# Twelve identity matmuls ahead of the first tile, contiguous first loads on two DMA queues, and the products with ahi first in every tile

## The chip, the cores and the metric

The kernel runs on one core of one Trainium2 chip. The metric is the device time of one execution in microseconds (us), as the median of several executions. Three executions of the kernel before took 613.04, 613.05 and 613.65 us. All durations below come from one profiled execution, which took 613.1 us. Its trace spans 611.3 us, so 1.8 us lie outside the span.

## The reference, cut to what matters

A graph layer with two branches and a residual, then a second graph layer. `adj` is a full 4096x4096 float32 matrix, and the features are 4096x128.

```
# layer 0, for (x, W1, b1) and for (x2, W2, b2)
ax = adj @ x;  h = ax + (1 + eps) * ax
for i in range(3): h = relu(h @ W[i].T + b[i])
x = layernorm(x + concat(h1, h2) @ Wm.T + bm)
# layer 1
A = adj + eye;  d = rsqrt(sum(A, axis=1))
x = layernorm(x + (d[:, None] * A * d[None, :] @ x) @ W.T + b)
```

So `adj` is multiplied once with x and x2 (256 columns) and once with the normalised x (128 columns).

## The kernel before

**Three products for one.** Every float32 operand is split in a rounded part and a rest. ScalarE (ACT) copies a tile `raw` (128x1024) to `ahi` in the rounded format fp32r (L489), VectorE (DVE) subtracts to get `alo` (L636). TensorE (PE) then adds up x_hi·ahi, x_hi·alo and x_lo·ahi (L344) in PSUM, 512 columns at a time. In layer 0 a tile is 2 branches x 3 products x 2 halves = 12 matmuls, in layer 1 it is 6.

**Order of the work.** The output columns are cut in four quarters of 1024. For each quarter, 32 tiles of `adj` (n = 0 to 31) are added up. Layer 0 runs quarters 0 to 3, then layer 1 runs quarters 0 to 3. The small dense layers of a quarter (L362, L373), the residual, the statistics and the norm are placed at fixed tiles of the next quarter. DVE also adds up row sums in layer 0 (L644, L647, L651).

**Rings.** `ahi` and `alo` have four places (SPLIT = 4): ACT may round tile n when PE has finished tile n - 4 (`block_used`). SyncE (SP) issues the loads of `adj`, two tiles in one DMA, when DVE has used the old ones.

**Waits of PE.** Before a tile PE waits for both `hi_ready` and `lo_ready`:

```
if not first:
    wait(pe, hi_ready, at)
    wait(pe, lo_ready, at)
...
w, a = ((whi, hi), (whi, lo), (wlo, hi))[k]
```

Middle tiles go through the branches b, then k = 0, 1, 2, then the halves c. Tiles 0 and 31 finish one PSUM bank after the other.

**The start.** SP issues x piece 0 (the first two blocks of x and of x2, 256 KB, L259), then the two halves of tile 0 of `adj` (256 KB each, L266), tile 1 (512 KB, L267), x piece 1, and so on. Pieces of x go through ACT (L464) and DVE (L622) and must be split before tiles 0, 2, 4, 8, 16 and 24; DVE splits piece 3 behind its work for tile 7. In tile 0 PE waits for `alo` of each half (L630). GpSimd (POOL) builds an identity (L899, L901), which layer 1 adds to `adj` (L791).

Of the kernel before, what the change touches and what calls it, by code (L numbers as in the profile page):

```python
# [27 lines left out]
P = 128  # L28
N = 4096
QUARTERS = 4  # L30
QW = N // QUARTERS
# [30 lines left out]
PE_MERGE = (10, 7)  # L62
PE_PROJECT = 1


# [25 lines left out]
X_PIECE_AT = {KB * q + k: i for i, (q, k, _) in enumerate(X_PIECES)}  # L91

X_AFTER = {1: 1, 3: 2, 7: 3, 12: 4, 20: 5}


def build(nc, a_t, x12, params, out):
    with ExitStack() as ctx:
# [103 lines left out]
        const_step = sem("const_step")  # L201
        const_ready = sem("const_ready")
        gain_ready = sem("gain_ready")
        whi_ready = sem("whi_ready")
        wlo_ready = sem("wlo_ready")

        as_f32 = lambda ap: ap.bitcast(F32)

        def wait(eng, s, value):
# [41 lines left out]
        def _(sp):  # L251
            def load_x(i):
                q, k0, k1 = X_PIECES[i]
                if q == 2:
                    sp.wait_ge(x_split, 2 * 3)
                if q == 3:
                    sp.wait_ge(x_split, 2 * 4)
                place = 2 * (q % 2)
                sp.dma_start(xn[:, place:place + 2, k0 * P:k1 * P],  # L259
                             x12[q][:, :, k0 * P:k1 * P]).then_inc(x_in[i], 16)  # L260


            load_x(0)
            for c in range(CH):
                cols = slice(c * CW, (c + 1) * CW)
                sp.dma_start(raw[:, 0, 0, cols], a_t[0][:, 0, cols]).then_inc(half_in[c], 16)  # L266
            sp.dma_start(raw[:, 0, 1], a_t[0][:, 1]).then_inc(raw_in[0], 16)  # L267
# [52 lines left out]
        def _(pe):  # L320
            def products(q, layer, n, stationary, first_wait):

                at = q * JB + (layer * QUARTERS * JB + n + 1)
                banks = [(b, c) for b in range(len(stationary)) for c in range(CH)]
                hi = [ahi[:, n % SPLIT, c * CW:(c + 1) * CW] for c in range(CH)]
                lo = [alo[:, n % SPLIT, c * CW:(c + 1) * CW] for c in range(CH)]
                first = isinstance(at, int) and at == 1
                if not first:
                    wait(pe, hi_ready, at)
                    wait(pe, lo_ready, at)  # L330
                if n in (0, JB - 1):

                    order = [(b, c, k) for b, c in banks for k in range(3)]
                else:
                    order = [(b, c, k) for b in range(len(stationary)) for k in range(3) for c in range(CH)]
                for b, c, k in order:
                    whi, wlo = stationary[b]
                    w, a = ((whi, hi), (whi, lo), (wlo, hi))[k]
                    bank = b * CH + c
                    if n == 0 and k == 0:  # L340
                        first_wait(bank)
                        if first and b == 0:
                            pe.wait_ge(lo_half if c == 0 else lo_ready, 1)
                    mm = pe.matmul(ps[bank][:, :], block_of(w, n), a[c],  # L344
                                   start=(n == 0 and k == 0), stop=(n == JB - 1 and k == 2))
                    if n == JB - 1 and k == 2 and (b, c) != banks[-1]:
                        mm.then_inc(ay_done if layer else ax_done, 1)
                mm.then_inc(block_used, 1)
# [40 lines left out]
            def layer0_quarter(q, before):  # L389
                def empty(bank):  # L390
                    if before is not None:
                        wait(pe, h_ready, before * (4 * M) + (bank + 1))
                for n in range(JB):
                    if before is None and n in X_PIECE_AT:
                        pe.wait_ge(x_split, 2 * (X_PIECE_AT[n] + 1))
# [14 lines left out]
            def last_products(q):  # L410

                for c in range(CH):
                    for n in range(JB - SPLIT, JB):
                        if c == 0:
                            pe.wait_ge(hi_ready, (QUARTERS + q) * JB + n + 1)
                            pe.wait_ge(lo_ready, (QUARTERS + q) * JB + n + 1)
# [10 lines left out]
            def layer1_quarter(q, before):  # L427
# [31 lines left out]
        def _(act):  # L459
            def round_x(i):  # L460
                q, k0, k1 = X_PIECES[i]
                act.wait_ge(x_in[i], 16)
                for b in range(2):
                    act.activation(x_hi_parts[b][:, q, k0 * P:k1 * P], xn[:, 2 * (q % 2) + b, k0 * P:k1 * P],  # L464
                                   ACT.Copy).then_inc(x_hi, 1)

            def round_a(q, layer, n):

                p = n // 2
                if layer == 0:  # L470
                    start = isinstance(q, int) and q == 0 and p < RAW
                    if start and n == 0:
                        for c in range(CH):
                            act.wait_ge(half_in[c], 16)
                            act.activation(ahi[:, 0, c * CW:(c + 1) * CW], raw[:, 0, 0, c * CW:(c + 1) * CW],
                                           ACT.Copy).then_inc((hi_half, hi_ready)[c], 1)
                        return
                    if start and n % 2 == 0:
# [112 lines left out]

            round_x(0)
            layer0_quarter(0, None)
# [23 lines left out]
        def _(dve):  # L617
            def split_x(i):
                q, k0, k1 = X_PIECES[i]
                for b in range(2):  # L620
                    dve.wait_ge(x_hi, 2 * i + b + 1)
# [228 lines left out]

            split_x(0)
            layer0_quarter(0, None)
# [34 lines left out]
        def _(pool):  # L887
# [5 lines left out]
            def norm_power(done, r=slice(0, KB)):  # L893
# [65 lines left out]
```

## Time and profile before

| what | value |
|---|---|
| median of 3 executions | 613.05 us (613.04 to 613.65) |
| profiled execution, its span | 613.1 us, 611.3 us |
| PE busy | 590.3 us, 97% of the span |
| DVE busy | 545.6 us, 89% |
| ACT busy | 368.2 us, 60% |
| DMA read from HBM | 139.14 MB |
| chain that ended last | PE 85%, DVE 10%, ACT 2%, issue 2%, DMA 1% |

Engines run side by side, so busy times don't add up. A matmul's busy time includes its passage through the array, and successive ones overlap: the distance from start to start is what a matmul costs. The chain goes back from the last instruction, each time to what released it.

### The profile page before, as it was taken

The numbers are of one execution on the slowest core, as the hardware profiler recorded it, in microseconds if no ns is written. First come the engines' busy times: TensorE is split into PE (matmuls) and PEld (weight loads), VectorE is DVE, ScalarE is ACT, GpSimd is POOL, SyncE is SP. The second block draws the span as 40 slices with busy tenths as digits, with TensorE's granted clock in tenths as the row PEclk, the third lists the DMA queues.
The fourth block names the chain that finished last, engine by engine and source line by source line (L and its number), as shares of the span: only waits on it lengthen the run. The fifth ranks groups of instructions, "written<-read, shape, count | busy, mean of one in ns | idle before, by whom it ended". The sixth has DMA issues, their size and how long they took to land.

```text
span 611.3 us, 7947 instructions
## 1 busy us (share of the span) xinstructions
PE 590.3 (97%) x2636; PEld 478.9 (78%) x2636; DVE 545.6 (89%) x696; ACT 368.2 (60%) x443; POOL 28.1 (5%) x30
## 2 busy tenths in 40 slices
PE   4999999999999999999999999999989999999994
PEld 3888888888888888888888888858668778778873
DVE  5999989998987997998899999876898998998994
ACT  5555337752545773453675254685767797797781
POOL 1000000001100000200000110001100100000011
PEclk9999999999999999999999999999999999999998
DMA  8967555334555433455533576583978999999800
GB/s 292 414 234 281 205 203 206 138 138 138 207 206 183 161 137 137 169 191 191 204 137 137 206 275 248 172 335 139 339 283 346 342 399 363 349 380 371 333 34 36
DMA packets 21289, 141.55 MB, mean 232 GB/s; under 512 B 2320, under 2 KB 2832, under 8 KB 5008
## 3 DMA queue, kind: packets, MB, share of 16 engines
q1 hardware_dynamic: 20544, 139.15, 61.1%
q10 hardware_dynamic: 720, 2.10, 0.9%
q8 instruction: 13, 0.21, 0.1%
q14 instruction: 12, 0.10, 0.0%
HBM read 139.14 MB, written 2.10 MB: 231 GB/s over the span
## 4 chain that ended last, share of the span: by engine, by line
PE 85%; DVE 10%; ACT 2%; issue 2%; DMA 1%; POOL 1%; POOLq 0%; SPq 0%; DVEq 0%; ACTq 0%
PE ps L344 75%; DVE alo L636 7%; PE pd L362 6%; PE pd L373 2%; PE pd L405 1%; ACT ahi L489 1%; DMA raw<-a_t 1%; DVE stats L708 1%; DVE z L801 1%; POOL rstd L896 1%; ACT outn L519 1%; PE ps L418 0%; DVE mv L716 0%; DVE raw L791 0%; DVE x1lo L775 0%
## 5 line engine op out<-in xcount | busy, mean ns | idle before, releaser
L489 ACT ACTIVATE ahi<-raw 128x1024 fp32r<-128x1024 f32 x255 | 267.7, 1059 | 209.3 <-PE ps L344 203.3
L636 DVE TENSOR_TENSOR alo<-raw,ahi 128x1024 fp32r<-128x1024 f32 x255 | 307.3, 1217 | 46.3 <-ACT ahi L489 45.3
L344 PE MATMUL ps<-ahi,x1hi 128*128 128x512 f32 x504 | 162.9, 399 | 12.1 <-DVE alo L630 8.0
L344 PE MATMUL ps<-ahi,x2s 128*128 128x512 f32 x512 | 159.9, 391 | 0.0
L344 PE MATMUL ps<-alo,x1hi 128*128 128x512 f32 x504 | 158.5, 391 | 0.0
L344 PE MATMUL ps<-ahi,x1lo 128*128 128x512 f32 x504 | 158.4, 391 | 0.0
L344 PEld LDWEIGHTS ps<-ahi,x1hi 128*128 128x128 f32 x504 | 92.5, 189 | 40.8 <-issue 14.1
L344 PEld LDWEIGHTS ps<-ahi,x2s 128*128 128x128 f32 x512 | 96.7, 189 | 20.3
L344 PEld LDWEIGHTS ps<-ahi,x1lo 128*128 128x128 f32 x504 | 94.9, 188 | 20.2
L344 PEld LDWEIGHTS ps<-alo,x1hi 128*128 128x128 f32 x504 | 95.0, 188 | 19.9
L344 PE MATMUL ps<-alo,x2s 128*128 128x512 f32 x256 | 80.6, 391 | 0.0
L647 DVE TENSOR_TENSOR rowsum<-rowsum,raw 128x1024 f32<-128x1024 f32 x60 | 72.9, 1215 | 0.0
L651 DVE TENSOR_TENSOR rowsum<-rowsum,raw 128x1024 f32<-128x1024 f32 x56 | 68.0, 1215 | 0.0
L344 PEld LDWEIGHTS ps<-alo,x2s 128*128 128x128 f32 x256 | 48.3, 189 | 10.1
L510 ACT ACTIVATE h<-pd,par 128x512 f32<-128x512 f32 x48 | 31.7, 677 | 1.2 <-PE pd L362 1.0
L896 POOL TENSOR_TENSOR rstd<-vareps,halves 128x8 f32<-128x8 f32 (+1 forms) x9 | 19.0, 2108 | 199.4 <-DVE vareps L723 199.4
L891 POOL TENSOR_TENSOR degpow<-degc,halves 128x8 f32<-128x8 f32 x4 | 6.6, 1638 | 378.5 <-DVE degpos L694 378.5
L656 DVE TENSOR_TENSOR hlo<-h,hhi 128x512 fp32r<-128x512 f32 x36 | 22.6, 683 | 0.0
L494 ACT ACTIVATE hhi<-h 128x512 fp32r<-128x512 f32 x36 | 22.1, 630 | 0.8
L373 PE MATMUL pd<-par,h 128*128 128x128 f32 x128 | 15.3, 278 | 0.0
L519 ACT ACTIVATE xn<-z,nshift,rstd 128x128 f32 (+1 forms) x32 | 13.9, 481 | 1.7 <-DVE nshift L728 1.7
L373 PEld LDWEIGHTS pd<-par,h 128*128 128x128 f32 x128 | 14.6, 192 | 0.0
(66 smaller groups left out, 265.7 us busy)
## 6 DMA issues: line engine op xcount, KB each, us to landing
raw<-a_t SPq DMA_DIRECT2D x124, 1024.0 KB, 4.8
raw<-a_t SPq DMA_DIRECT2D x7, 512.0 KB, 8.9
xn<-x SPq DMA_DIRECT2D x3, 1024.0 KB, 7.9
out<-outn ACTq DMA_DIRECT2D x3, 512.0 KB, 3.9
par<-params SPq DMA_DIRECT2D x1, 708.0 KB, 14.3
xn<-x SPq DMA_DIRECT2D x2, 256.0 KB, 4.8
raw<-a_t SPq DMA_DIRECT2D x2, 256.0 KB, 5.1
xn<-x SPq DMA_DIRECT2D x1, 512.0 KB, 8.2
```

The costliest lines, as they stand in the source:

```text
L344: mm = pe.matmul(ps[bank][:, :], block_of(w, n), a[c], start=(n == 0 and k == 0), stop=(n == JB - 1 and k == 2))
L362: mm = pe.matmul(pd[:, m, :], w[:, at:at + P], a[:, m, :], start=(k == 0), stop=(k == len(passes) - 1))
L373: mm = pe.matmul(merged[:, k, :], h[:, CH * b + k // 4, (k % 4) * P:(k % 4 + 1) * P], par[:, WM_AT + b * P:WM_AT + (b + 1) * P], start=(k ...
L489: act.activation(ahi[:, n % SPLIT, :], raw_tile(layer, n), ACT.Copy).then_inc(hi_ready, 1)
L494: act.activation(hhi[:, m, :], h[:, m, :], ACT.Copy).then_inc(hhi_ready, 1)
L510: act.activation(h[:, m, :], pd[:, m, :], ACT.Relu, bias=par[:, at:at + 1]).then_inc(h_ready, 1)
L519: i = act.activation(dst(k), z[:, k, :], ACT.Identity, scale=rstd[:, k:k + 1], bias=nshift[:, k:k + 1])
L636: dve.tensor_tensor(alo[:, n % SPLIT, :], raw_tile(layer, n), as_f32(ahi[:, n % SPLIT, :]), ALU.subtract).then_inc(lo_ready, 1)
L647: dve.tensor_tensor(rowsum[:, :], rowsum[:, :], tile, ALU.add).then_inc(rowsum_step, 1)
L651: dve.tensor_tensor(to[:, :], rowsum[:, :], tile, ALU.add).then_inc(raw_used, 1)
L656: dve.tensor_tensor(hlo[:, m, :], h[:, m, :], as_f32(hhi[:, m, :]), ALU.subtract).then_inc(hlo_ready, 1)
L896: pool.tensor_tensor(rstd[:, r], vareps[:, r], halves[:, r], ALU.pow).then_inc(rstd_ready, 1)
```

## The change

- SP now begins with the two halves of tile 0, out of an array `head` in which each half is contiguous. ACT issues x piece 0 itself, on its own queue. All pieces of x are contiguous in HBM.
- POOL builds the identity first; PE multiplies it with itself 12 times (float32, 128 columns) into a PSUM bank that is overwritten later.
- ACT and DVE take the x part of piece 0, half 0 of tile 0, the x2 part, then half 1.
- In all tiles, the products with `alo` (k = 1) come last, and PE waits for `lo_ready` only ahead of the first of them. In tile 0, and in tiles 0 and 31 of every quarter, this is per bank. The last four tiles of the last quarter (`last_products`) take the order x_hi·ahi, x_lo·ahi, x_hi·alo for each half.

```diff
+PE_WARM = 12
...
-            load_x(0)
             for c in range(CH):
-                cols = slice(c * CW, (c + 1) * CW)
-                sp.dma_start(raw[:, 0, 0, cols], a_t[0][:, 0, cols]).then_inc(half_in[c], 16)
+                sp.dma_start(raw[:, 0, 0, c * CW:(c + 1) * CW], head[c]).then_inc(half_in[c], 16)
...
+                if n in (0, JB - 1):
+                    order = [(b, c, k) for b, c in banks for k in (0, 2, 1)]
+                else:
+                    order = [(b, c, k) for b in range(len(stationary)) for k in (0, 2) for c in range(CH)]
+                    order += [(b, c, 1) for b in range(len(stationary)) for c in range(CH)]
                 if not first:
                     wait(pe, hi_ready, at)
-                    wait(pe, lo_ready, at)
...
+                lo_seen = False
                 for b, c, k in order:
+                    if k == 1 and not lo_seen and not first:
+                        wait(pe, lo_ready, at)
+                        lo_seen = True
...
                         if first and b == 0:
-                            pe.wait_ge(lo_half if c == 0 else lo_ready, 1)
+                            pe.wait_ge((hi_half, hi_ready)[c], 1)
+                        if first and bank == CH:
+                            pe.wait_ge(x_split, 2)
+                    if first and b == 0 and k == 1:
+                        pe.wait_ge((lo_half, lo_ready)[c], 1)
...
-                        for k, (w, a) in enumerate(((x1hi, ahi), (x1hi, alo), (x1lo, ahi))):
+                        for k, (w, a) in enumerate(((x1hi, ahi), (x1lo, ahi), (x1hi, alo))):
+                            if c == 0 and k == 2:
+                                pe.wait_ge(lo_ready, (QUARTERS + q) * JB + n + 1)
...
+            pe.wait_ge(warm_ready, 1)
+            for k in range(PE_WARM):
+                pe.matmul(pd[:, 3, 0:P], identity[:, :], identity[:, :], start=True, stop=True)
             layer0_quarter(0, None)
...
+                            if c == 0:
+                                round_x(0, (1,))
...
-            round_x(0)
+            _, k0, k1 = X_PIECES[0]
+            act.dma_start(xn[:, 0:2, k0 * P:k1 * P], x_piece(0)).then_inc(x_in[0], 16)
+            round_x(0, (0,))
             layer0_quarter(0, None)
...
+                        if c == 0:
+                            split_x(0, (1,))
...
-            pool.memset(halves[:, :], -0.5).then_inc(const_ready, 1)
             pool.memset(identity[:, :], 0.0).then_inc(const_step, 1)
...
-                               base=0, pattern=[[-1, P]], channel_multiplier=1).then_inc(const_ready, 1)
+                               base=0, pattern=[[-1, P]], channel_multiplier=1).then_inc(warm_ready, 1)
+            pool.wait_ge(warm_ready, 1)
+            pool.memset(halves[:, :], -0.5).then_inc(const_ready, 2)
```

## Rows read from the trace of the kernel before

**Rows 1.** The page's part 1: busy us, share and instructions.

```profile
PE 590.3 (97%) x2636; PEld 478.9 (78%) x2636; DVE 545.6 (89%) x696; ACT 368.2 (60%) x443; POOL 28.1 (5%) x30
```

**Rows 2.** Chain in order of time, layer 0: start us, us, what.

```profile
1.45 5.07 DMA raw<-a_t
...
8.04 100.96 PE ps L344 x432
...
140.08 68.05 PE ps L344 x300
```

**Rows 3.** Timeline of PE, tile 0: start us, us, engine line op.

```profile
8.60 0.63 PE L344 MATMUL ps<-alo,x1hi 128*128 128x512 f32 x1
...
13.29 0.93 PE L344 MATMUL ps<-ahi,x1hi 128*128 128x512 f32 x2
```

**Rows 4.** Timeline of ACT and DVE, first tiles.

```profile
4.11 0.42 ACT L464 ACTIVATE x1hi<-xn 128x256 fp32r<-128x256 f32 x1 [2.09 <-DMA xn<-x]
...
8.49 1.06 ACT L489 ACTIVATE ahi<-raw 128x1024 fp32r<-128x1024 f32 x1 [0.67 <-DMA raw<-a_t]
...
9.58 1.23 DVE L636 TENSOR_TENSOR alo<-raw,ahi 128x1024 fp32r<-128x1024 f32 x1 [1.03 <-ACT ahi L489]
...
28.50 1.21 DVE L622 TENSOR_TENSOR x2s<-xn,x2s 128x1024 fp32r<-128x1024 f32 x1
...
29.63 1.21 DVE L636 TENSOR_TENSOR alo<-raw,ahi 128x1024 fp32r<-128x1024 f32 x1
```

**Rows 5.** Groups of instructions of DVE, 13.29 to 98 us: busy, mean ns, idle before.

```profile
L636 DVE TENSOR_TENSOR alo<-raw,ahi 128x1024 fp32r<-128x1024 f32 x33 | 40.0, 1214 | 1.8 <-ACT ahi L489 1.7
```

**Rows 6.** Timeline of DVE and PE, the first dense layer in quarter 1.

```profile
105.58 1.29 DVE L656 TENSOR_TENSOR hlo<-h,hhi 128x512 fp32r<-128x512 f32 x2
...
108.83 0.39 PE L362 MATMUL pd<-hhi,whi 128*128 128x512 f32 x1
```

**Rows 7.** Windows of the start: busy by engine, PEclk, DMA share, GB/s.

```profile
4.00:5.00 1.00, 0.00 (x0) 0.00 (x0) 0.44 (x2) 0.72 (x2) 0.12 (x2) 1.00 0.51 98
...
8.00:9.00 1.00, 0.96 (x2) 0.83 (x3) 0.55 (x1) 0.51 (x1) 0.00 (x0) 1.00 1.06 402
```

**Rows 8.** Timeline of ACT and of SP's queue, first instructions.

```profile
0.74 0.66 SPq L259 DMA_DIRECT2D xn<-x  x1
0.74 1.28 ACT L464 ACT_TABLE_LOAD   x1 [0.74 <-PEq L953]
1.45 1.05 SPq L266 DMA_DIRECT2D raw<-a_t  x2
```

**Rows 9.** Timeline: the identity on POOL, and float32 matmuls of 128 columns.

```profile
1.22 0.29 POOL L901 TENSOR_SCALAR_AFFINE_SELECT identity<-identity 128x128 f32<-128x128 f32 x1 [0.24 <-POOL identity L899]
...
416.78 3.82 PE L373 MATMUL pd<-par,h 128*128 128x128 f32 x32
420.36 0.48 PE L344 MATMUL ps<-ahi,x1hi 128*128 128x512 f32 x1
```

**Rows 10.** Timeline of PE, layer 1: tiles of quarters 0, 1 and 2.

```profile
446.44 0.73 PE L344 MATMUL ps<-ahi,x1hi 128*128 128x512 f32 x2 [1.57 <-DVE x1lo L775]
...
448.81 0.70 PE L344 MATMUL ps<-ahi,x1hi 128*128 128x512 f32 x2 [0.70 <-DVE alo L636]
...
497.73 0.70 PE L344 MATMUL ps<-ahi,x1hi 128*128 128x512 f32 x2
...
535.01 0.70 PE L344 MATMUL ps<-ahi,x1hi 128*128 128x512 f32 x2 [0.23 <-DVE alo L636]
535.55 0.62 PE L344 MATMUL ps<-alo,x1hi 128*128 128x512 f32 x2
```

**Rows 11.** Timeline of DVE in quarter 2 of layer 1.

```profile
513.53 1.23 DVE L636 TENSOR_TENSOR alo<-raw,ahi 128x1024 fp32r<-128x1024 f32 x1 [0.87 <-ACT ahi L489]
...
533.61 1.25 DVE L636 TENSOR_TENSOR alo<-raw,ahi 128x1024 fp32r<-128x1024 f32 x1
```

**Rows 12.** Chain in order of time, end of the last quarter.

```profile
595.99 1.23 DVE alo L636
```

More of the change, by code:

```diff
@@ L91, with build @@
 X_PIECE_AT = {KB * q + k: i for i, (q, k, _) in enumerate(X_PIECES)}
+X_PIECE_START = [2 * P * P * sum(k1 - k0 for _, k0, k1 in X_PIECES[:i]) for i in range(len(X_PIECES))]
 X_AFTER = {1: 1, 3: 2, 7: 3, 12: 4, 20: 5}
-def build(nc, a_t, x12, params, out):
+def build(nc, a_t, head, x12, params, out):
     with ExitStack() as ctx:
@@ L202, in build @@
         const_ready = sem("const_ready")
+        warm_ready = sem("warm_ready")
         gain_ready = sem("gain_ready")
@@ L207, in build, with x_piece @@
         as_f32 = lambda ap: ap.bitcast(F32)
+        def x_piece(i):
+            _, k0, k1 = X_PIECES[i]
+            at = X_PIECE_START[i]
+            return x12[at:at + P * 2 * (k1 - k0) * P].rearrange("(p t w) -> p t w", p=P, t=2)
         def wait(eng, s, value):
@@ L258, in load_x @@
                 place = 2 * (q % 2)
-                sp.dma_start(xn[:, place:place + 2, k0 * P:k1 * P],
-                             x12[q][:, :, k0 * P:k1 * P]).then_inc(x_in[i], 16)
-            load_x(0)
+                sp.dma_start(xn[:, place:place + 2, k0 * P:k1 * P], x_piece(i)).then_inc(x_in[i], 16)
             for c in range(CH):
-                cols = slice(c * CW, (c + 1) * CW)
-                sp.dma_start(raw[:, 0, 0, cols], a_t[0][:, 0, cols]).then_inc(half_in[c], 16)
+                sp.dma_start(raw[:, 0, 0, c * CW:(c + 1) * CW], head[c]).then_inc(half_in[c], 16)
             sp.dma_start(raw[:, 0, 1], a_t[0][:, 1]).then_inc(raw_in[0], 16)
@@ L327, in products @@
                 first = isinstance(at, int) and at == 1
+                if n in (0, JB - 1):
[3 more added lines that the diff above has]
+                    order += [(b, c, 1) for b in range(len(stationary)) for c in range(CH)]
                 if not first:
                     wait(pe, hi_ready, at)
-                    wait(pe, lo_ready, at)
[L331 to L335, printed above, removed]
+                lo_seen = False
                 for b, c, k in order:
+                    if k == 1 and not lo_seen and not first:
+                        wait(pe, lo_ready, at)
+                        lo_seen = True
                     whi, wlo = stationary[b]
@@ L342, in products @@
                         if first and b == 0:
-                            pe.wait_ge(lo_half if c == 0 else lo_ready, 1)
+                            pe.wait_ge((hi_half, hi_ready)[c], 1)
[3 more added lines that the diff above has]
+                        pe.wait_ge((lo_half, lo_ready)[c], 1)
                     mm = pe.matmul(ps[bank][:, :], block_of(w, n), a[c],
-                                   start=(n == 0 and k == 0), stop=(n == JB - 1 and k == 2))
-                    if n == JB - 1 and k == 2 and (b, c) != banks[-1]:
+                                   start=(n == 0 and k == 0), stop=(n == JB - 1 and k == 1))
+                    if n == JB - 1 and k == 1 and (b, c) != banks[-1]:
                         mm.then_inc(ay_done if layer else ax_done, 1)
@@ L394, in layer0_quarter @@
                     if before is None and n in X_PIECE_AT:
-                        pe.wait_ge(x_split, 2 * (X_PIECE_AT[n] + 1))
+                        pe.wait_ge(x_split, 2 * X_PIECE_AT[n] + (2 if n else 1))
                     products(q, 0, n, ((x1hi, x1lo), (x2hi, x2lo)), empty)
@@ L459, in _, with round_x @@
         def _(act):
-            def round_x(i):
+            def round_x(i, pair=(0, 1)):
                 q, k0, k1 = X_PIECES[i]
                 act.wait_ge(x_in[i], 16)
-                for b in range(2):
+                for b in pair:
                     act.activation(x_hi_parts[b][:, q, k0 * P:k1 * P], xn[:, 2 * (q % 2) + b, k0 * P:k1 * P],
@@ L617, in _, with split_x @@
         def _(dve):
-            def split_x(i):
+            def split_x(i, pair=(0, 1)):
                 q, k0, k1 = X_PIECES[i]
-                for b in range(2):
+                for b in pair:
                     dve.wait_ge(x_hi, 2 * i + b + 1)
@@ L849, in layer1_quarter @@
                         add_identity(q, n + AHEAD)
-            split_x(0)
+            split_x(0, (0,))
             layer0_quarter(0, None)
@@ L946 @@
     ], axis=1))
+    head = np.ascontiguousarray(a_t[0][:, 0].reshape(P, CH, CW).transpose(1, 0, 2))
+    x12 = np.stack([x["x"].reshape(QUARTERS, P, QW), x["L0_gnn_x2"].reshape(QUARTERS, P, QW)], axis=2)
     arrays = {
         "a_t": a_t,
-        "x12": np.ascontiguousarray(np.stack([x["x"].reshape(QUARTERS, P, QW),
-                                              x["L0_gnn_x2"].reshape(QUARTERS, P, QW)], axis=2)),
+        "head": head,
+        "x12": np.concatenate([x12[q][:, :, k0 * P:k1 * P].reshape(-1) for q, k0, k1 in X_PIECES]),
         "params": params,
```

1 line of the change is left out of this document (removed).

## The prediction

> **What bounds the kernel now.** I read the page first: PE is busy for 97% of the span [rows 1], so only three things can bring much: a cheaper matmul, an earlier first one, or fewer gaps. The chain in order of time then says where PE is not the bound. In layer 0 it is PE in one piece from 8.04 us on. A tile of 12 matmuls costs 12 x 68.05/300 = 2.722 us [rows 2], and the 100.96 us of 432 matmuls are 36 tiles, 98.0 us at that pace and 3.0 us more.
>
> The 3.0 us are at the start. The first matmuls stand 0.426 us apart (eleven from 8.60 to 13.29), which is 512 columns at 1.2 GHz; from 13.3 us on they go at 0.227 us, near 512 columns at 2.4 GHz [rows 2, 3]. The column of the granted clock shows 1.00 all along [rows 7], so here the distance between matmuls is what tells the level. Ahead of 8.04 us PE waits for the load of half 0 (1.45 + 5.07 = 6.52 us [rows 2]), its rounding and its `alo`.
>
> In layer 1 a tile has 6 matmuls and 1.36 us, and DVE has 1.13 us (28.50 to 29.63 [rows 4]) for `alo` and more work beside it: it falls behind, and PE waits for `alo` in each of the four quarters. The timeline of PE shows this as tiles further apart than 1.36 us: the one at 446.44 is 2.37 us ahead of the next [rows 10].
>
> **The start, part by part.** (1) Identity matmuls. The identity is there at 1.51 us [rows 9], PE starts at about 1.56. Sixteen such float32 matmuls (32 records) take 420.36 - 416.78 = 3.58 us at the high level [rows 9], 0.224 each; at the low one, by 0.427/0.227, 0.42. Twelve are 5.1 us: they end at 6.6 us. Before, PE worked some 5.3 us at the low level before it changed (8.04 to 13.3), so after these 5.1 us one or two matmuls of tile 0 may still be slow, 0.2 us each. The first real matmul is at 6.6 us, if its data is there.
>
> (2) Its data. Half 0 now goes out first, at 0.74 instead of 1.45 us [rows 8]; x piece 0 goes out on ACT's queue in parallel. Before, the piece issued at 0.74 was at ACT by 4.11 [rows 4], half 0 only by 6.52. I expect both between 4.1 and 5.5, and `ahi` of the half within a rounding of that (1.06 us for a whole tile [rows 4]): in time for 6.6. Should ACT load its table (1.28 us [rows 8]) ahead of the issue, the piece comes 1.3 us later, at 5.4, and still in time. The split order (x, half 0, x2, half 1) serves the order in which PE asks; it costs no instruction more and lies beside the identity matmuls. Without that cover it would be worth what half 0 gains.
>
> (3) What comes due next. With tile 0 at 6.6 and 2.722 us a tile, PE would be at tile 8 at 6.6 + 21.8 = 28.4 us. But DVE works without a pause from `alo` of tile 1 (9.58) on, and is through with piece 3 of x, which tile 8 needs, at 28.50 + 1.21 = 29.71 us [rows 4]. In 13.29 to 98 us it waits for 1.8 us in all, the most of it at the end of the quarter [rows 5], so a faster PE doesn't make it faster. Before, tile 8 started at 8.04 + 100.96 - 28 x 2.722 = 32.8 us. So the start is worth 32.8 - 29.7 = 3.1 us with DVE's times as they were, and 4.4 us at most (PE's own 28.4). Behind tile 8, DVE has 2 x 1.13 = 2.27 us for a tile against PE's 2.72 and two more pieces of 2.27 us. Its `alo` of tile 13 would end at 30.84 + 6 x 2.27 = 44.5, and PE asks for it behind the 8 products with `ahi`, at 29.71 + 5 x 2.722 + 1.82 = 45.1; at tile 21 it is 64.9 against 66.9: no further wait. Into quarter 1 DVE brings 1.8 us of its own catch-up against PE's 3.1; the dense layer there had 2 us to spare behind DVE's `hlo` (106.87 to 108.83 [rows 6]). It holds.
>
> (4) How much earlier DVE begins: `ahi` of tile 1 waited for its load until 8.49 us [rows 4]. The load goes out 0.7 us earlier. Between 4 and 5 us the DMA moved only 98 GB/s, against 402 later [rows 7]; I estimate 1.3 us earlier if that hole, which begins before 4 us, is filled. If the hole stays, the bytes ahead of it are the same 768 KB and it comes at the same time; if ACT is still at half 1, 0.3 later. The range is -0.3 to +1.3 us (PE's own 28.4 allows all of it). I take 0.5: the earlier issue counts for most, the hole stays. Sum of the start: 3.1 + 0.5 = 3.6 us.
>
> What the skill says about (4): by the Trainium skill, "DMA: Bandwidth & Descriptors", section "Issuing engines are not separate DMA queues", DMAs from several engines run on the same 16 DMA engines, and starting them on two saves the sequencer's time alone. The same page has one descriptor for one contiguous run of the last dimension, and the destination's runs of x piece 0 are 1 KB before and after. By the two rules the bytes ahead of tile 1 take as long as before, and the start's sum would be 3.1 us, where I have 3.6. No row here shows two queues at once.
>
> **Products with ahi first.** No instruction is added; one wait moves into the tile. In layer 0, after the start, PE never waits [rows 2]: nothing to gain. In layer 1 a tile that waited for `alo` with all 6 matmuls now waits with 2 of them. Where `alo` is late, the tile ends 4 x 0.227 = 0.91 us earlier for the same `alo`; and if PE then runs on to the end of the quarter, all that follows (its releases of the ring, the rounding, the next quarter's DVE work) is 0.91 us earlier. It counts once a quarter, at the last tile that DVE holds up; DVE's own late stretch begins, by its trace, at an `ahi` that waits for PE [rows 11], so it moves along.
> - Quarter 0: tile 24 waits for y's rest (x1lo) until 446.4, which stays. Tile 25 waits for `alo` till 448.7 [rows 10]: 0.9 us.
> - Quarter 1: tiles slip by 0.1 to 0.3 us from the tenth on; the last one held up starts at 497.73 [rows 10]: 0.95 us (0.91 and part of a restart).
> - Quarter 2: `alo` ends at 534.86, PE starts at 535.01 [rows 10, 11]; before, tile and wait end at 536.5, now 535.5: 0.95 us.
> - Quarter 3: DVE is late up to the very last `alo` (597.2 [rows 12]). Then PE had three products for half 0 and now has one: 0.45 us.
>
> Sum 3.25 us. The bounds: 1.8, if half of it is lost to later waits that now come to light; 3.9, if the restarts of earlier held-up tiles (a stalled tile's first two matmuls take 0.54 us instead of 0.455 [rows 10]) go as well.
>
> POOL's new order and `halves` later are hidden: `halves` is needed far behind quarter 0. SP loses one issue, ACT wins one, of 0.66 us [rows 8], while it has nothing to round: its cover is the wait for the piece itself.
>
> Total 3.6 + 3.25 = 6.85 us: the profiled execution's 613.1 becomes 606.2, and as it stands 0.05 us from the median, so does the median.
>
> **Rivals.**
> - *Loads no earlier*: the 768 KB ahead of tile 1 take as long from two queues and out of contiguous rows as they do now, DVE begins at 9.58 as before, the start is worth 3.1, the time is 606.7. For it: the DMA streams at some 400 GB/s soon after [rows 7]. Against it: the hole, in which the engines are busy for half of the time [rows 7], so something else than bytes sets it. 20%. (The two rules of the Trainium skill's page "DMA: Bandwidth & Descriptors" named above speak for this rival.)
> - *The clock isn't up for tile 0.* Then tile 0 takes 5.25 us from 6.6 (as from 8.04 to 13.29 [rows 2, 3]), tile 8 starts at 6.6 + 5.25 + 7 x 2.722 = 30.9, the start is worth 1.9: 607.9. For it: identity matmuls are not the same work as the others, and a gap may come between them and tile 0. Against it: 5.1 us of work is what the change took before. 12%.
> - *No gain in layer 1*: DVE's lateness is a matter of its throughput, and PE only waits inside the tile instead of ahead of it, with the ring slowed elsewhere: 613.05 - 3.6 = 609.5. For it: DVE runs without pause for 20 us from 513.53 on. Against it: behind 535.01 PE runs on unheld. 10%.
> - *Slower*: the wait inside each tile breaks the chain of weight loads and matmuls even when `alo` is there. Price: 0.085 us (0.54 - 0.455 [rows 10]) in each of 255 tiles, 21.7 us, less 6.85: 627.9. It decides from 6.85/255 = 27 ns a tile on. Against it: the two waits between tiles today cost nothing where they are met (12 matmuls a tile at 68.05/300 each, waits included [rows 2]). 5%.
> - *Given back*: DVE's smaller lead holds up the nine dense layers of layer 0's quarters; at 0.7 us each, 6.3 in all, the time stays at 612.5. Against it: the 2 us to spare [rows 6]. 3%.
>
> **How the numbers follow.** The forecast (605.0 to 607.3 around 606.2) has 48%, and 2% I leave for more than 8.3 us of gain. The range of 604.5 to 608.8 goes from both upper bounds (4.4 + 3.9 is 604.8, some rounding) to both lower ones (2.8 + 1.8 is 608.5) and takes in the first two rivals; outside are 10 + 5 + 3% and crumbs. A difference of 0.2%, 1.2 us, is about what a measurement of this kernel tells from no change. Faster: 48 + 2 + 20 + 12 + 10 = 92%; same: 3%; slower: 5%.
>
> **What would show it.** Right: float32 matmuls from 1.56 to about 6.6 us, then real ones 0.227 us apart at once; tile 8 near 29.2 us behind a wait for x2s; layer 0's quarters still 99.1 us long; in layer 1 waits for `alo` inside tiles, quarters 1 and 2 each about 1 us shorter, and one product of half 0 behind the last `alo`. Wrong: real matmuls at 0.427 us; matmuls further apart at each third of a tile; waits of PE for DVE in the first tiles that are longer than its head start.

## The result, and the profile after

Six executions of the changed kernel gave a median of 609.12 us (608.07 to 610.05), six of the kernel before 612.78 us (611.93 to 613.65). The ratio is 0.9942, 95% interval 0.9928 to 0.9956: faster, by 3.7 us. The prediction said 606.2 with a range of 604.5 to 608.8, so the sign is right, but the gain is about half of the 6.85 us forecast, and the time lies above the range. The profiled execution took 610.05 us, the slowest of the six; its span is 608.2 us, 3.1 us less than before.

The page of the changed kernel, part 1, answers to [rows 1]. PE has 24 records more (the identity matmuls) and is busy for 3.7 us more:

```profile
PE 594.0 (98%) x2660; PEld 485.0 (80%) x2660; DVE 544.9 (90%) x696; ACT 367.5 (60%) x443; POOL 28.2 (5%) x30
```

The start, in the timeline of PE (start us, us, engine line op), answers to [rows 3] and [rows 6]:

```profile
1.53 5.23 PE L463 MATMUL pd<-identity 128*128 128x128 f32 x24 [1.53 <-POOL identity L925]
6.51 0.48 PE L359 MATMUL ps<-ahi,x1hi 128*128 128x512 f32 x1
6.83 0.39 PE L359 MATMUL ps<-ahi,x1lo 128*128 128x512 f32 x1
...
9.86 0.73 PE L359 MATMUL ps<-ahi,x1hi 128*128 128x512 f32 x2 [0.34 <-ACT ahi L510]
...
30.02 0.73 PE L359 MATMUL ps<-ahi,x1hi 128*128 128x512 f32 x2 [0.18 <-DVE x2s L645]
...
106.32 0.39 PE L377 MATMUL pd<-hhi,whi 128*128 128x512 f32 x1
```

The identity matmuls run from 1.53 to about 6.6 us, tile 0 starts at 6.51 us at the full rate, and tile 1 at 9.86 instead of 13.29. Tile 8, at 30.02 us, waits for `x2s` of piece 3, as foreseen. The first dense layer, the milestone of [rows 6], is at 106.32 instead of 108.83 us: 2.5 us gained.

Why tile 8 isn't earlier stands in the timeline of ACT and DVE (answers to [rows 4] and [rows 8]):

```profile
0.75 0.65 ACTq L614 DMA_DIRECT2D xn<-x  x1
1.43 1.28 ACT L483 ACT_TABLE_LOAD   x1 [1.43 <-PEq L981]
4.44 0.42 ACT L483 ACTIVATE x1hi<-xn 128x256 fp32r<-128x256 f32 x1 [1.73 <-DMA xn<-x]
4.76 0.61 ACT L494 ACTIVATE ahi<-raw 128x512 fp32r<-128x512 f32 x1
...
8.75 1.06 ACT L510 ACTIVATE ahi<-raw 128x1024 fp32r<-128x1024 f32 x1 [2.55 <-DMA raw<-a_t]
...
28.75 1.21 DVE L645 TENSOR_TENSOR x2s<-xn,x2s 128x1024 fp32r<-128x1024 f32 x1
```

ACT issues its load first and its table follows, so x piece 0 is there at 4.44 us, within the bounds of the prediction. Half 0 is rounded at 4.76 us instead of 6.54. But the load of tile 1 lets `ahi` start at 8.75 us, where it was 8.49, although it was issued earlier. DVE's whole row behind it, up to `x2s` of piece 3 (28.50 before, 28.75 now), moved later with it. The windows of the start (busy by engine, PEclk, DMA share, GB/s) answer to [rows 7]: the hole in the DMA traffic is still there, it only lies later. Within it the DMA engines are now busy 99% and 86% of the time and still move only 176 and 200 GB/s.

```profile
5.00:6.00 1.00, 1.00 (x7) 1.00 (x7) 0.91 (x2) 1.00 (x3) 0.00 (x0) 1.00 0.99 176
6.00:7.00 1.00, 1.00 (x7) 0.96 (x7) 1.00 (x3) 0.20 (x1) 0.00 (x0) 1.00 0.86 200
```

Layer 1, quarter 0, around tile 24, in the timeline of PE (answers to [rows 10]):

```profile
440.63 0.73 PE L359 MATMUL ps<-alo,x1hi 128*128 128x512 f32 x2 [0.62 <-DVE alo L661]
443.92 1.22 PE L359 MATMUL ps<-ahi,x1hi 128*128 128x512 f32 x2 [2.56 <-DVE x1lo L800]
444.94 1.06 PE L359 MATMUL ps<-ahi,x1lo 128*128 128x512 f32 x2
...
450.06 0.64 PE L359 MATMUL ps<-ahi,x1lo 128*128 128x512 f32 x2
```

The first weight load of tile 24 in the timeline, before and now; the number in brackets is how long weight loads had stood still:

```profile
446.44 0.30 PEld L344 LDWEIGHTS ps<-ahi,x1hi 128*128 128x128 f32 x2 [2.01 <-DVE x1lo L775]
...
443.92 0.50 PEld L359 LDWEIGHTS ps<-ahi,x1hi 128*128 128x128 f32 x2 [3.00 <-DVE x1lo L800]
```

And the windows of the changed kernel's stretch (PEclk, the granted clock, is the third number from the end):

```profile
440.00:444.00 4.00, 0.82 (x4) 0.38 (x3) 3.06 (x4) 4.00 (x5) 0.00 (x0) 0.91 0.81 289
444.00:446.00 2.00, 2.00 (x5) 1.63 (x6) 2.00 (x2) 0.31 (x1) 0.00 (x0) 0.50 0.41 172
446.00:448.00 2.00, 2.00 (x6) 1.54 (x6) 2.00 (x3) 1.05 (x1) 0.00 (x0) 0.50 0.50 74
448.00:450.00 2.00, 2.00 (x6) 1.60 (x5) 1.54 (x2) 0.56 (x2) 0.00 (x0) 0.50 0.84 344
450.00:452.00 2.00, 2.00 (x10) 1.59 (x9) 1.22 (x1) 1.24 (x2) 0.00 (x0) 0.98 1.02 414
```

Here is where the gain went. Tile 24 starts 2.5 us earlier than before (443.92 against 446.44), still with the start's whole gain. But PE's idle time ahead of it grew from 1.57 to 2.56 us, the pause of the weight loads from 2.01 to 3.00 us, and behind it the granted clock is 0.50 for 6 us, that is 1.2 instead of 2.4 GHz (before, it was 1.00 throughout this stretch). The first window's 0.91 puts the fall at about 443.3 us, inside the pause. The 14 matmuls from 443.92 to 450.06 us take 6.14 us; at 0.227 each, with the restart of 0.1, they would take 3.3. That is 2.85 us, and it eats the 0.9 that quarter 0 was to gain and 1.9 of the start's.

The rest is in the chain in order of time (answers to [rows 12]), first the changed kernel:

```profile
458.00 3.02 PE ps L359 x12
...
504.60 3.02 PE ps L359 x12
...
550.76 3.02 PE ps L359 x12
...
597.56 1.14 DVE z L826 x4
```

and before:

```profile
458.60 3.02 PE ps L344 x12
...
506.17 3.02 PE ps L344 x12
...
553.31 3.01 PE ps L344 x12
...
600.60 1.14 DVE z L801 x4
```

The groups of 12 are the starts of quarters 1, 2 and 3; `z` stands behind the last matmuls. The lead over the kernel before is thus 2.51 us at the first dense layer, 2.52 at tile 24, 0.60 at quarter 1, 1.57 at quarter 2, 2.55 at quarter 3, and 3.04 at the end.

### The profile page after: what moved, and what is told of

Read it like the earlier page. It is cut to its first block, busy times and chain, and to the rows that moved or that the text cites. A ratio compares the mean times of both kernels' runs of the same rounds, so it can differ in the third digit from the quotient of the medians.

```text
span 608.2 us, 7750 instructions
## 1 busy us (share of the span) xinstructions
PE 594.0 (98%) x2660; PEld 485.0 (80%) x2660; DVE 544.9 (90%) x696; ACT 367.5 (60%) x443; POOL 28.2 (5%) x30
## 4 chain that ended last, share of the span: by engine, by line
issue 70%; PE 19%; DVE 5%; POOL 3%; ACT 2%; POOLq 0%; DVEq 0%; ACTq 0%
PE ps L359 18%; DVE alo L661 4%; ACT ahi L510 1%; POOL degpow L916 1%; POOL rstd L921 1%; PE pd L420 1%; ACT outn L540 1%; ACT xn L540 0%; DVE z L826 0%; PE ps L434 0%; DVE stats L733 0%; POOL same_place L934 0%; DVE yt L795 0%; DVE x1lo L800 0%; POOLq L99 0%
## 5 line engine op out<-in xcount | busy, mean ns | idle before, releaser
L359 PE MATMUL ps<-ahi,x2s 128*128 128x512 f32 x512 | 138.3, 390 | 0.0
L359 PEld LDWEIGHTS ps<-ahi,x1hi 128*128 128x128 f32 x504 | 94.5, 190 | 27.1 <-DVE x1lo L800 3.0
L540 ACT ACTIVATE outn<-z,nshift,rstd 128x128 f32<-128x128 f32 x28 | 12.1, 481 | 4.4 <-DVE nshift L753 4.4
```

Source lines behind the costliest of these rows:

```text
L359: mm = pe.matmul(ps[bank][:, :], block_of(w, n), a[c], start=(n == 0 and k == 0), stop=(n == JB - 1 and k == 1))
L540: i = act.activation(dst(k), z[:, k, :], ACT.Identity, scale=rstd[:, k:k + 1], bias=nshift[:, k:k + 1])
```

## The experiments

Theory: the longer pause ahead of tile 24 makes the clock fall, and the fall costs 2.8 us. Rivals: the order of the products itself lowers the rate behind the pause; the start's gain is lost elsewhere; DVE, not the clock, holds quarter 0. Each ran beside the kernel before on the same chip, whose median was 612.41 us (12 executions) for 1 to 4, 612.24 (11) for 5 to 8 and 612.68 (15) for 9 to 12. All of them compute the whole reference.

**1. The old order up to tile 24 of quarter 0**, against the changed kernel:

```diff
+elif layer == 1 and isinstance(q, int) and q == 0 and n <= 24:
+    order = [(b, c, k) for b in range(len(stationary)) for k in range(3) for c in range(CH)]
...
-lo_seen = False
+lo_seen = layer == 1 and isinstance(q, int) and q == 0 and n <= 24
+if lo_seen:
+    wait(pe, lo_ready, at)
```

> The changed kernel, with the old order of products in tiles 1 to 24 of quarter 0 of layer 1 and the new order everywhere else. Theory (gap): with ahi first PE finishes tile 23 earlier and stands idle longer ahead of tile 24, which waits for x1lo; the pause of the weight loads was 2.0 us before and is 3.0 us in the changed kernel, and behind it the granted clock is 0.50 for some 6 us. With the old order the pause is 2.0 us again, the clock stays at 1.00, and the time is 612.8 - 2.5 (start) - 0.9 - 1.0 - 1.0 - 0.5 (one term for each quarter of layer 1) = 606.9. Rival (waits inside tiles cost, or the order itself): only a quarter of layer 1 is given back, under 1 us, 608.3 to 609.1, and the clock drops again. Rival (the new start shifts the clock's windows): the drop stays, 609.1.

606.12 us (605.65 to 607.34), ratio 0.9902 [0.9887, 0.9916]. In PE's timeline the pause is as before, and so is the rate behind it:

```profile
442.36 0.73 PE L363 MATMUL ps<-ahi,x1hi 128*128 128x512 f32 x2 [1.58 <-DVE x1lo L804]
442.93 0.62 PE L363 MATMUL ps<-alo,x1hi 128*128 128x512 f32 x2
```

By the ratios, giving up the new order in 24 tiles makes the kernel 2.4 us faster than the changed one. The time is 0.8 us below the 606.9 expected; neither rival occurred.

**2. The changed kernel with the pause filled** by ten identity matmuls, order untouched:

```diff
+PE_FILL = 10
...
+if before is None and n == 3 * KB:
+    for k in range(PE_FILL):
+        pe.matmul(pd[:, 3, 0:P], identity[:, :], identity[:, :], start=True, stop=True)
```

> The changed kernel with ten more identity matmuls on PE between tile 23 and tile 24 of quarter 0 of layer 1, 10 x 0.224 = 2.2 us of work inside the 3.0 us pause. Nothing else is changed, the order stays ahi first. Theory (gap): the pause is under 1 us, the clock stays at 1.00, tile 24 starts where it did (443.9 us) and the time is 606.9 to 607.1. Rival (the order or its waits cost): the time stays at 609.1. If the identity matmuls ended later than x1lo, tile 24 would start later by what they overrun.

606.98 us (605.52 to 607.49), 0.9902 [0.9889, 0.9915]. PE's timeline:

```profile
441.38 2.39 PE L454 MATMUL pd<-identity 128*128 128x128 f32 x20
444.11 0.73 PE L360 MATMUL ps<-ahi,x1hi 128*128 128x512 f32 x2 [0.33 <-DVE x1lo L804]
444.68 0.62 PE L360 MATMUL ps<-ahi,x1lo 128*128 128x512 f32 x2
```

The time is the one expected. Tile 24 waits for the same `x1lo` and starts 0.2 us later than in the changed kernel, yet all is at full rate behind it. Work that computes nothing saves 2.4 us by the ratios, so neither the order nor DVE is to blame, only PE's idleness.

**3. The order alone**, on the kernel before (its loads, its split, no identity matmuls; all lines of the diff that deal with k and `lo_ready`):

```diff
-order = [(b, c, k) for b in range(len(stationary)) for k in range(3) for c in range(CH)]
+order = [(b, c, k) for b in range(len(stationary)) for k in (0, 2) for c in range(CH)]
+order += [(b, c, 1) for b in range(len(stationary)) for c in range(CH)]
...
-    wait(pe, lo_ready, at)
...
-pe.wait_ge(lo_half if c == 0 else lo_ready, 1)
+pe.wait_ge((hi_half, hi_ready)[c], 1)
```

> The kernel before with the new order of products and its waits alone; loads, start and POOL as before. Theory (gap): start 0, quarter 0 of layer 1 loses 1.9 us to the clock as in the changed kernel, quarters 1 to 3 win 1.0 + 1.0 + 0.5: 612.8 + 1.9 - 2.5 = 612.2, within 0.2% of before, and the granted clock shows 0.50 behind tile 24. Rival (the clock falls only together with the new start): 612.8 - 3.4 = 609.4.

609.37 us (608.69 to 610.41), 0.9951 [0.9938, 0.9964]. The clock did fall, yet the expectation missed by 2.8 us, for two reasons that its trace shows: the order brings a gain at the start that I hadn't counted (2.3 us at the first dense layer), and fewer products ran at the low level than in the changed kernel's trace (6, in 2.7 us, against 14), which cost about 1.5 us less. The rival's time came out without its reason. PE's timeline:

```profile
7.12 0.76 PE L353 MATMUL ps<-ahi,x1hi 128*128 128x512 f32 x1 [7.12 <-ACT ahi L485]
...
9.81 0.76 PE L353 MATMUL ps<-ahi,x2s 128*128 128x512 f32 x2
10.41 0.39 PE L353 MATMUL ps<-alo,x2s 128*128 128x512 f32 x1
...
444.14 1.22 PE L353 MATMUL ps<-ahi,x1hi 128*128 128x512 f32 x2 [2.56 <-DVE x1lo L785]
...
446.87 0.70 PE L353 MATMUL ps<-ahi,x1hi 128*128 128x512 f32 x2
```

Tile 0 waits for `ahi` and no longer for `alo`: 7.12 instead of 8.04 us. And in this execution the clock was up at about 10.1 us, 3.0 after the first product, where it took over 5 before.

**4. The start alone**, the changed kernel with the old order and its old waits everywhere (the diff of experiment 3 the other way round):

> The changed kernel with the old order of products in all tiles: the new loads, queues, split order and identity matmuls stay. Theory (gap): layer 1 is as before, the pause ahead of tile 24 is 2.0 us, the clock stays at 1.00, and the start gives its 2.5 us, less 0.2 since PE now waits for alo in the first tiles: 610.3 to 610.5. Rival (the new start brings the clock drop): 612.5 or more.

610.74 us (609.82 to 611.69), 0.9972 [0.9961, 0.9983]. Close to what was foreseen; no fall. By the ratios the two halves of the change bring 1.7 and 3.0 us alone and 3.6 together. In these traces they overlap at the start: the first dense layer is earlier by 2.3 us with either half and by 2.5 with both. But the order's share of that isn't there each time (experiments 9 and 11), and the shorter fall in experiment 3's trace is part of its 3.0.

**5. No identity matmuls** (changed kernel):

```diff
-PE_WARM = 12
+PE_WARM = 0
```

> The changed kernel without its twelve identity matmuls ahead of tile 0. Theory (DVE caps the start): PE begins tile 0 at about 5.4 us, when ahi of half 0 is there, on the low clock, and ends it near 10; tile 8 still waits for piece 3 of x, which DVE finishes at 28.4 to 30.1 us whatever PE does. The time is that of the changed kernel, 609.1 within 0.5 us. Rival (the warm clock is what earns the start): tile 0 costs 2.5 us more and the time is 611.3 to 611.6.

609.11 us (608.15 to 609.40), 0.9942 [0.9929, 0.9955], the changed kernel's ratio to the last digit. PE's timeline shows a slow tile 0 that nevertheless is through in time:

```profile
5.63 0.77 PE L359 MATMUL ps<-ahi,x1hi 128*128 128x512 f32 x1 [5.63 <-ACT ahi L494]
...
10.07 0.62 PE L359 MATMUL ps<-ahi,x1hi 128*128 128x512 f32 x2
```

Tile 0 starts 0.9 us earlier than behind the identity matmuls, tile 1 0.2 later, and the first dense layer is at 105.56, 0.76 us earlier; the load of tile 1 had landed 0.75 us earlier too (`ahi` at 8.00).

**6. One queue**: x piece 0 back on SP ahead of the halves of tile 0, still contiguous.

```diff
+load_x(0)
 for c in range(CH):
     sp.dma_start(raw[:, 0, 0, c * CW:(c + 1) * CW], head[c]).then_inc(half_in[c], 16)
...
-act.dma_start(xn[:, 0:2, k0 * P:k1 * P], x_piece(0)).then_inc(x_in[0], 16)
```

> The changed kernel with x piece 0 issued by SP again, ahead of the two halves, so that all loads go out on one queue; the arrays stay contiguous and the identity matmuls stay. Theory (DVE caps the start): half 0 comes at 6.3 to 6.5 us as it did before and PE starts tile 0 near 7.1, but the load of tile 1 comes no later than with two queues (ACT had it at 8.3 to 8.5 us with the old loads, and at 7.2 to 8.9 us in four executions with the new ones), so DVE is as early and the time is 609.1 within 0.7 us. Rival (the second queue earns the start): 610 or more.

608.39 us (607.75 to 610.71), 0.9941 [0.9925, 0.9957]: the second queue brings nothing. ACT's timeline:

```profile
3.66 0.42 ACT L484 ACTIVATE x1hi<-xn 128x256 fp32r<-128x256 f32 x1 [1.64 <-DMA xn<-x]
4.67 0.63 ACT L495 ACTIVATE ahi<-raw 128x512 fp32r<-128x512 f32 x1 [0.59 <-DMA raw<-head]
```

Half 0 is there at 4.67 us with the order of issues as before, where it was 6.54. The time is as expected, but this is not: I had expected the half at 6.3 to 6.5. So it is its contiguous rows in HBM that brought it forward. The piece of x ahead of it, contiguous too, isn't the reason: in experiment 9, with the old loads, the piece was at ACT at the same 3.66 us, and half 0 at 6.79. The Trainium skill, "DMA: Bandwidth & Descriptors", section "Issuing engines are not separate DMA queues", says that starting DMAs on several engines saves only the time to issue them; this run agrees.

**7. The rest of y first**: the changed kernel, but DVE splits y (`x1lo`) ahead of tile 24's `alo` instead of behind it, and adds the bias to `xn` four tiles later.

```diff
                 dve.tensor_tensor(..., ALU.subtract).then_inc(y_ready, 1)
+
+            def y_base(g):
                 dve.tensor_tensor(quarter(xn, g), quarter(xn, g), bias_rows(BO_AT), ALU.add).then_inc(base_ready, 1)
...
+if before is None and n == DVE_SPLIT_Y[QUARTERS - 1]:
+    split_y(QUARTERS - 1)
 split_a(q, 1, n)
...
+if n == DVE_SPLIT_Y[QUARTERS - 1] + 4:
+    y_base(QUARTERS - 1)
```

> The changed kernel, with DVE's work at tile 24 of quarter 0 of layer 1 in another order: x1lo, for which PE waits ahead of tile 24, comes before alo of tile 24, and the bias on xn moves behind tile 28. Theory (gap): x1lo is there at 441.7 instead of 443.9 us, PE's pause is under 1 us, the clock stays at 1.00, and with ahi first PE covers the later alo. Against the run with the filled pause (607.0, tile 24 at 444.1) it wins 2.2 to 2.4 us: 604.7. Rival (the alo of the next tiles then comes late, so DVE's order only moves the wait): 606.5 to 607.

604.86 us (604.74 to 605.26), 0.9877 [0.9863, 0.9891]. Timeline of DVE and PE:

```profile
440.00 1.23 DVE L800 TENSOR_TENSOR x1lo<-yt,x1hi 128x1024 fp32r<-128x1024 f32 x1
...
441.28 0.73 PE L359 MATMUL ps<-ahi,x1hi 128*128 128x512 f32 x2 [0.48 <-DVE x1lo L800]
```

As expected: the pause is short, the clock stays up, and tile 24 itself starts 2.6 us earlier than in the changed kernel, 0.6 of it from the start.

**8. The same, and pieces of x ahead of the row sums** in layer 0, quarter 0:

```diff
 split_a(q, 0, n)
+if before is None and n in X_AFTER:
+    split_x(X_AFTER[n])
 sum_rows(q, n)
```

> The kernel of e7_y_rest_first, in which DVE also splits a piece of x ahead of the row sum of the same tile in quarter 0 of layer 0 instead of behind it. Theory (DVE caps the start at the pieces of x): piece 3 is ready 1.13 us earlier, PE is held by alo of tile 8 instead, which lets 0.7 us of it through: 604.0. Rival (loads or alo are the cap): as e7_y_rest_first, 604.7.

604.30 us (603.99 to 604.74), 0.9865 [0.9851, 0.9880]: the best version, 7.9 us ahead of the kernel before. Its interval overlaps that of experiment 7, and the 0.7 us between them lies between expectation and rival; the traces below show the same 0.7 us. `x2s` of piece 3 starts at 27.73 us, and no tile near 8 waits for it any more; tile 8 waits a little for its own `alo` instead (its first product with `alo` starts at 31.27 us, 0.3 later than at the full rate).

**9. Order and y first, with the old start** (experiments 3 and 7 together, on the kernel before):

> The kernel before with two edits: the new order of products, and DVE's order at tile 24 as in e7_y_rest_first (x1lo first, the bias behind tile 28). Loads, queues and start are the old ones, there are no identity matmuls. Theory (the start's and the order's gains overlap in the same first tiles): with ahi first PE starts tile 0 at 7.1 us and runs unheld, e3_order_alone had tile 24 at 444.1 as the changed kernel had (443.9); so this is e7's time plus 0.2 to 0.5: 605.1 to 605.4. Rival (the new start is worth its 1.7 us, as in e4_start_alone, beside the order too): 606.5.

606.74 us (606.37 to 607.21), 0.9905 [0.9890, 0.9919]. The expectation missed and its rival hit: I had read experiment 3 as saying that the new loads and identity matmuls add nothing to the order. PE's timeline shows the difference from experiment 3. Here the clock stays low through tile 0:

```profile
7.56 0.77 PE L353 MATMUL ps<-ahi,x1hi 128*128 128x512 f32 x1 [7.56 <-ACT ahi L485]
...
12.82 0.79 PE L353 MATMUL ps<-ahi,x1hi 128*128 128x512 f32 x2
```

**10. A longer pause in the old order**, on the kernel before: the bias of the last quarter goes ahead of `x1lo`.

```diff
+if g == QUARTERS - 1:
+    dve.tensor_tensor(quarter(xn, g), quarter(xn, g), bias_rows(BO_AT), ALU.add).then_inc(base_ready, 1)
 ... # x1lo
-dve.tensor_tensor(quarter(xn, g), quarter(xn, g), bias_rows(BO_AT), ALU.add).then_inc(base_ready, 1)
+if g < QUARTERS - 1:
+    dve.tensor_tensor(quarter(xn, g), quarter(xn, g), bias_rows(BO_AT), ALU.add).then_inc(base_ready, 1)
```

> The kernel before with one edit: at tile 24 of quarter 0 of layer 1 DVE adds the bias to xn (1.13 us) ahead of x1lo instead of behind it, so that PE stands idle 1.13 us longer ahead of tile 24, with the old order of products. Theory (gap): the pause of the weight loads grows from 2.0 to about 3.1 us and the granted clock falls to 0.50 behind it with the old order too, for 3 to 6 us; the time grows by 1.1 less 1.0 (the next alo then comes right behind) plus 1.2 to 2.7: 613.6 to 615. Rival (the fall has to do with the order of the products or its waits): the clock stays at 1.00 and the time is 612.3 to 612.6.

614.97 us (612.06 to 615.74, 10 executions), 1.0034 [1.0020, 1.0048]: slower than before. The weight load of tile 24 in the timeline, and the windows behind it:

```profile
447.58 0.50 PEld L344 LDWEIGHTS ps<-ahi,x1hi 128*128 128x128 f32 x2 [3.16 <-DVE x1lo L777]
```

```profile
448.00:450.00 2.00, 2.00 (x6) 1.52 (x6) 2.00 (x3) 0.00 (x0) 0.00 (x0) 0.50 0.14 16
450.00:452.00 2.00, 2.00 (x9) 1.64 (x8) 1.23 (x2) 1.06 (x1) 0.00 (x0) 0.86 0.83 328
```

The old order falls too, once its pause is as long. Eight of the ten executions took 614.7 to 615.7 us with a mean clock of 0.991 to 0.993; the other two took 612.06 and 612.68 with 0.996, as kernels without a fall show (0.995 to 0.997). By the same sign one of the six executions of experiment 6 (608.06 us, 0.995) may have escaped as well.

**11. All but the new start** (experiment 9 and the x pieces of 8):

> The kernel of e9_order_and_y_old_start, in which DVE splits pieces of x ahead of the row sums, as in e8_y_and_x_first. Against e8 it tells what the new start is worth when DVE's pieces of x no longer cap it. Theory: here PE itself sets tile 8 (from 7.1 us on with a cold tile 0, about 30.4 us), so the earlier piece brings nothing: 605.1 to 605.4 as e9, against e8's 604.3; the new start is worth 0.7 to 1.1 us. Rival (the cap is DVE here too): 604.5.

606.26 us (605.60 to 606.52), 0.9896 [0.9882, 0.9911]. Missed by 1 us for the same reason as 9: against experiment 8 (0.9865) the new start is worth 1.9 us.

**12. The changed kernel again:**

> The changed kernel once more, unedited, on the chip of the other three, to see what its time and its two traces share. Theory (gap): the pause ahead of tile 24 is 3.0 us again and the clock falls again; how long it stays low differs between executions (2.6 us in e3, 6 us in the first trace), so the times spread over about 2 us, 608 to 610. Rival (the first result was a bad draw): 606 to 607 and no fall.

608.83 us (607.60 to 609.14), 0.9937 [0.9924, 0.9949]. Same pause; in PE's timeline matmuls are at the full rate at first, 0.427 us apart by 445.7, and fast again by 448.9:

```profile
443.93 0.74 PE L359 MATMUL ps<-ahi,x1hi 128*128 128x512 f32 x2 [2.57 <-DVE x1lo L800]
...
445.71 1.05 PE L359 MATMUL ps<-ahi,x1hi 128*128 128x512 f32 x2
...
448.86 0.63 PE L359 MATMUL ps<-ahi,x1lo 128*128 128x512 f32 x2
```

**All traces side by side.** Three milestones cut each profiled execution: the first dense layer (D), the start of layer 1's quarter 2 (Q2), and `z` behind the last products. A difference of milestones doesn't carry what happened earlier. All in us:

| kernel | `ahi` of tile 1 | D | D to Q2 | Q2 to z | pause of weight loads at tile 24 |
|---|---|---|---|---|---|
| before | 8.49 | 108.83 | 397.34 | 94.43 | 2.01 |
| 10: before, longer pause | 8.73 | 108.81 | 398.95 | 94.47 | 3.16 |
| 4: start alone | 7.76 | 106.55 | 397.32 | 94.38 | 2.02 |
| changed | 8.75 | 106.32 | 398.28 | 92.96 | 3.00 |
| 12: changed again | 8.74 | 106.30 | 397.13 | 92.93 | 3.00 |
| 5: no identity matmuls | 8.00 | 105.56 | 398.31 | 92.98 | 3.00 |
| 6: one queue | 8.28 | 105.84 | 396.95 | 93.00 | 3.00 |
| 3: order alone | 8.29 | 106.53 | 396.77 | 92.98 | 3.00 |
| 1: old order to 24 | 7.18 | 104.75 | 395.45 | 92.94 | 2.02 |
| 2: pause filled | 8.88 | 106.49 | 395.40 | 93.03 | 0.52 |
| 7: y first | 8.18 | 105.75 | 393.68 | 93.02 | 0.92 |
| 8: y and x first | 8.86 | 105.75 | 393.61 | 92.92 | 0.92 |
| 9: order, y first, old start | 8.71 | 108.19 | 393.60 | 92.96 | 0.92 |
| 11: 9 and x first | 8.32 | 107.12 | 393.68 | 93.02 | 0.92 |

- From D to Q2, the order is worth 1.9 us (397.3 to 395.4) where the clock holds. With a pause of 3.0 us or more all six traces show a fall, and it costs 1.4 to 2.9 us; the eight with 2.02 us or less show none.
- From Q2 to the end, the order is worth 1.4 to 1.5 us in every kernel that has it.
- With the new start and the new order (changed, 1, 2, 5, 6, 7, 12), D lies 97.56 to 97.61 us behind `ahi` of tile 1: PE's clock in tile 0, the identity matmuls and the queue don't enter, only DVE's row of work from that load on. Experiment 8 cuts that row to 96.89.
- With the old start the distance is 98.2 to 100.3 us: there PE, whose clock comes up late, is behind DVE. D is 106.5, 107.1 and 108.2 us in 3, 11 and 9, 107.3 on average, and 105.9 over the seven with the new start. So beside the order the new start is worth 1.4 us on average: 0.2 against experiment 3, where the clock came up early, and 2.4 between 9 and 7.

## Why the prediction was off

**The step that failed** is the one on quarter 0: "tile 24 waits for y's rest (x1lo) until 446.4, which stays. Tile 25 waits for `alo` till 448.7 [rows 10]: 0.9 us." The wait for `x1lo` did stay. But tile 23 now ends 4 matmuls sooner behind the same `alo`, and `x1lo` comes at the same distance behind that `alo`, so the 0.9 us reappears as pause: weight loads stand still for 3.00 us instead of 2.01. In that pause the clock falls. Shown: experiment 1 takes the longer pause away, 2 fills it, 7 brings `x1lo` forward, and in each the fall and 2.4 to 4.0 us (by the ratios) go; experiment 10 makes the fall with the old order. Measured, the term is -1.9 us instead of +0.9. With the clock held up the 0.9 is there: in 1 and 2, D to Q2 is 1.9 us shorter than before, the 0.9 and 0.95 forecast for quarters 0 and 1. The Trainium skill, "TensorE: Matmul & The Clock Gate", section "HAM oscillation — how this bites in real kernels", describes a kernel that waits for data between groups of matmuls and begins each group at the low clock. The traces agree in kind: 14 products of the changed kernel from tile 24 on run at it behind a pause of 3.00 us. The prediction used the clock for the start and didn't put the same question to the gap that its own edit lengthens.

**The start.** Forecast 3.6 us, in the trace 2.5, below my lower bound of 2.8. The cap by DVE's x pieces at tile 8 is shown: [rows 4]'s `x2s` end of 29.71 came as 29.96, and the table's constant 97.6 us says the same for seven traces. Two terms were off. The 0.5 us for earlier loads was -0.26 in this trace: the load of tile 1 came no earlier, as the rival *Loads no earlier* had it, and even a little later. And from tile 8 to D the old kernel needed 76.0 us, the new one 76.3, of which the restart behind the wait (0.1) is a part; I had put nothing there. Over the traces `ahi` of tile 1 starts between 7.18 and 8.88 us with the new start (nine traces, 8.29 on average) and between 8.29 and 8.73 with the old one (five, 8.51 on average). So against the 8.49 of before the term is -0.4 to +1.3, and 0.2 on average; that the one trace compared above had -0.26 is the luck of an execution.

**Quarters 1, 2 and 3** were forecast at 0.95, 0.95 and 0.45 us, and measured 0.97, 0.98 and 0.49. The mechanism (a tile held up for `alo` ends four products sooner, counted once a quarter at the last such tile) fits there in kind and size. Experiment 4, without the order, has none of it (397.32 and 94.38 us in the table, as before).

**Identity matmuls and clock.** Right as described in the changed kernel's trace (from 1.53 to 6.6 us, tile 0 at once at some 0.23 us), but not in every one: in experiment 7's, with the same start, the first two products of tile 0 still took 0.57 and 0.43 us (the rival *The clock isn't up for tile 0*, in part). The 5.3 us that the prediction gave the low level before are also too few: the pair of matmuls at 13.29 us is still slow in part, and only from 14.06 on are they 0.227 apart. What the identity matmuls are worth beside the rest is nothing that the runs tell (experiment 5): a slow tile 0 delayed tile 1 by 0.2 us, and behind it tile 8 follows DVE's x piece in any case (it started at 29.27 us, the piece was through at 29.22).

**The rivals.** *No gain in layer 1* named 609.5, close to the result by luck, for a reason that didn't hold: quarters 1 to 3 gained 2.4 us in full. *Slower* and *given back* didn't occur. The right rival, a gap that outlasts the clock, was missing. Sum, in the profiled executions: 2.51 - 1.91 + 0.97 + 0.98 + 0.49 = 3.04 us, the milestones' lead at `z`.

**What stays open.** By the granted clock in windows of 1 us, the low level lasts 3.4 us in the traces of 3, 6, 10 and 12 and 6.8 us in those of the changed kernel and of 5, at nearly the same pause. It begins 0.7 us ahead of tile 24 in the changed kernel's trace and 1.2 us behind its start in 12's. No record tells what decides either, nor why two executions of experiment 10 escaped. The six executions of the changed kernel divide in two groups, 608.07 to 608.54 us at a mean clock of 0.993 and 609.71 to 610.05 at 0.990 or 0.991, as a short and a long fall would give; the five of experiment 12 don't divide as clearly. No run has a pause between 2.02 and 3.00 us, so where between them a fall becomes possible isn't known.

Which part of the new start, its loads, its waits or the identity matmuls, keeps PE close behind DVE in experiments 7 and 8 wasn't tried one by one beside them. Without the identity matmuls (5) the distance was 97.56 us too, which speaks for the loads, but in that execution the clock came up early, some 3.4 us after the first product.

## What to carry to other kernels

When an edit lets TensorE finish sooner in front of a wait whose end doesn't move, add the gain to that pause and ask what the clock will do behind it; shortening the pause from its other side (here: the waited-for subtraction ahead of two others on VectorE) pays twice. A start that is bound by the second engine's backlog is worth what that backlog moves, here to within 0.05 us: find the one load at its head before speeding anything else up. Cutting each trace at the same few milestones separates such effects where medians, with 1 to 2 us of spread, can't.

## What the runs showed of the hardware

- After weight loads had stood still for 3.0 to 3.2 us, the granted clock went to 0.50 in all six traces, in one of them only 1.2 us after work had begun again, and 2.7 to 6.1 us of work ran at it; by the mean clock, two of ten executions of one kernel escaped. None of the eight traces with a pause of 2.02 us or less at that place shows it.
- From the first product, or identity matmul, to the full rate took 3.0 us (experiment 3), 3.4 (5), 4.1 (11), over 5 (before, 9) and 6.1 (7, from the first identity matmul). Until then the granted clock's column shows 1.00 while matmuls are 0.427 us apart.
- A 256 KB load with contiguous rows in HBM let `ahi` start at 4.67 us (experiment 6) where the strided one gave 6.35 to 6.79 (before, 3, 9, 10, 11), issued at the same place in the same queue.
- The load of tile 1 let `ahi` start over a range of 1.7 us (7.18 in experiment 1, 8.88 in 2) with the same start, and D followed it to within 0.05 us.
